# Two attentions in one kernel: rows of the first group loaded earlier, first chunks of scores and their maxima moved into the projection turns ahead, order of the first projection changed

## What is computed

```
block 1:  h = layernorm(x);  q, k, v = h @ Wqkv;  q, k = rotate(q, k)
          a = softmax(causal(q k^T / sqrt(8)));  x = x + (a v) Wo
          x = x + gelu(layernorm(x) W1 + b1) W2 + b2
block 2:  q, k, v = x Wq + bq, ...;  q, k = rotate_half(q, k)
          a = softmax(q k^T / sqrt(8))  (not causal);  x1 = layernorm(x + (a v) Wo + bo)
          top 2 of 8 experts, gelu MLP of width 512 each;  out = layernorm(x1 + moe)
```

## Time and profile before

| | |
|---|---|
| runs | 1601.58, 1604.15, 1609.94 us, median 1604.15 |
| the profiled execution's own time | 1594.96 us |
| its span | 1593.1 us, 36099 instructions |
| mean granted TensorE clock | 0.939 |
| busy: PE, DVE, ACT, POOL | 87%, 76%, 72%, 30% |
| chain that ended last, by engine | PE 42%, DVE 10%, DMA 4%, issue 4%, ACT 3%, POOL 3% |
| DMA queue of SP | 120864 packets, 130.77 MB |

### The profile page before, as it was taken

How to read it: one execution, slowest core, us unless ns; L and a number is a source line. 1 busy time by engine, 2 the same in 40 slices (tenths; PEclk the granted TensorE clock), 3 DMA queues, 4 the chain that set the end, 5 groups by cost and what they waited for, 6 DMA issues and landing times.

```text
span 1593.1 us, 36099 instructions
## 1 busy us (share of the span) xinstructions
PE 1386.2 (87%) x13425; PEld 602.7 (38%) x13425; DVE 1215.1 (76%) x1846; ACT 1143.0 (72%) x2357; POOL 480.9 (30%) x786
## 2 busy tenths in 40 slices
PE   5669999999998899369999999999989998999840
PEld 2323343334333566112222222322322235889730
DVE  6788888888883466799999999999999952523334
ACT  7618888888888566129999998899879986434321
POOL 5413333333333566200000002100222344323455
PEclk9959999999999999659999999999999999999975
DMA  4622112121112353301333331112001405688741
GB/s 139 195 86 75 64 46 70 44 76 52 68 46 88 116 169 116 128 6 48 108 137 125 109 95 37 43 57 91 30 35 48 134 30 152 189 247 258 234 126 56
DMA packets 130256, 158.26 MB, mean 99 GB/s; under 512 B 17313, under 2 KB 103329, under 8 KB 129825
## 3 DMA queue, kind: packets, MB, share of 16 engines
q1 hardware_dynamic: 120864, 130.77, 26.2%
q0 software_dynamic: 9216, 25.18, 4.6%
HBM read 90.90 MB, written 68.96 MB: 100 GB/s over the span
## 4 chain that ended last, share of the span: by engine, by line
PE 42%; DVE 10%; DMA 4%; issue 4%; ACT 3%; POOL 3%; SPq 1%; ACTq 0%; POOLq 0%; DVEq 0%
PE bank L628 16%; PE banks L613 9%; DVE row_max L664 7%; PE banks L585 6%; PE banks L1524 3%; PE banks L1514 3%; DMA sorted_in<-v_all,slots 2%; POOL probs L1332 2%; PE banks L1416 2%; ACT o_sums L724 1%; DMA parts<-sorted_in 1%; PE banks L337 1%; DMA qk_parts<-parts 1%; ACT front L2015 1%; PE bank L1423 0%
## 5 line engine op out<-in xcount | busy, mean ns | idle before, releaser
L664 DVE TENSOR_REDUCE row_max<-banks 128x2 f32<-128x1024 f32 (+3 forms) x896 | 933.7, 1105 | 60.8 <-PE banks L585 32.9
L709 ACT ACTIVATE probs<-banks 128x512 f32<-128x512 f32 (+3 forms) x1792 | 875.7, 553 | 116.4 <-PE banks L613 93.8
L628 PE MATMUL bank<-probs,v_ones 128*32 128x256 f32 (+2 forms) x6656 | 523.2, 386 | 11.9 <-ACT o_sums L724 10.8
L585 PE MATMUL banks<-k_work,q_work 48*128 48x512 bf16 (+3 forms) x1792 | 358.4, 376 | 66.9 <-DVE row_max L664 47.8
L613 PE MATMUL banks<-q_work,k_work 51*128 51x512 bf16 (+3 forms) x1792 | 376.5, 367 | 10.9 <-ACT probs L709 9.9
L613 PEld LDWEIGHTS banks<-q_work,k_work 51*128 51x128 bf16 x1792 | 104.4, 93 | 380.0 <-ACT probs L709 344.4
L628 PEld LDWEIGHTS bank<-probs,v_ones 128*32 128x32 f32 x6656 | 133.7, 108 | 258.1 <-ACT probs L709 174.2
L750 POOL DMA_DIRECT2D heads_out<-o_sums x64 | 36.3, 567 | 470.2 <-ACT o_sums L724 470.2
L2092 ACT ACTIVATE rope<-banks,expert 128x256 f32<-128x256 f32 x184 | 72.0, 474 | 113.5 <-PE banks L1514 113.5
L770 POOL TENSOR_SCALAR_AFFINE_SELECT probs<-probs 128x256 f32<-128x256 f32 x256 | 103.6, 408 | 127.3 <-ACT probs L709 126.5
L585 PEld LDWEIGHTS banks<-k_work,q_work 48*128 48x128 bf16 x1792 | 90.2, 95 | 125.0 <-DVE row_max L664 91.2
(11 more groups left out here) (195 smaller groups left out, 1042.5 us busy)
## 6 DMA issues: line engine op xcount, KB each, us to landing
expert<-expert_rows SPq DMA_DIRECT2D x46, 578.0 KB, 4.4
qk_parts<-parts SPq DMA_DIRECT2D x64, 256.0 KB, 2.7
heads_out<-o_sums POOLq DMA_DIRECT2D x64, 256.0 KB, 3.8
sorted_in<-front SPq DMA_DIRECT2D x21, 512.0 KB, 5.9
q_work<-qk_parts SPq DMA_DIRECT2D x64, 128.0 KB
k_work<-qk_parts SPq DMA_DIRECT2D x64, 128.0 KB
parts<-sorted_in SPq DMA_DIRECT2D x46, 128.0 KB, 4.3
q_work<-qk_parts SPq DMA_DIRECT2D x64, 64.0 KB
```

The source lines that it names most:

```text
L585: last = pe.matmul(to[:, par, 0:width], q[r:r + M0, pair, qt * P:(qt + 1) * P], k[r:r + M0, pair, kh * G:kh * G + width], start=True, stop ...
L628: last = pe.matmul(bank[7][32 * j:32 * j + 32, c0 + c1:c0 + c1 + w], v_ones[i % QB][:, kt, j, :], prob_slots[:, (e + j) % RING, c1:c1 + w] ...
L664: dve.tensor_reduce(row_max[:, :, pair, qt, kh], self.buf_of("chunk", g, c)[:, :, 0:width], AX.X, ALU.max).then_inc(s["chunk_max"], 1)
L709: act.activation(prob_slots[:, e % RING, 0:width], self.ring_bank("exp", e)[:, 0:width], ACT.Exp, scale=SCALE).then_inc(s["exps"], 1)
```

## The change

The chunk and its maximum become methods, so that the stage ahead can call them. EARLY says how many chunks of group 0 it makes: 5 of 24 in the first attention, 6 of 32 in the second. The rest of the first LEAD ones stay where they were.

```diff
+EARLY = {1: 5, 2: 6}
+        LAST_HALVES = (GROUPS - 1, 2 * GROUPS - 1)
+                self.turned = (hT, yT) if a == 1 else (hT, hT)
+            def bank_of(self, which, n):
+                return bank[WO_BANK if n in LAST_HALVES else which]
             def input(self, act, n):
-                if n:
-                    act.wait_ge(s["v"], n)
                 if a == 1:
-                    act.activation(hT[:, :], bank[T_BANK], ...
+                    if n >= 2:
+                        act.wait_ge(s["v"], n - 1)
+                    act.activation(self.turned[n % 2][:, :], self.bank_of(T_BANK, n), ...
-                for c in range(LEAD):
-                    chunk(0, c)
+                for c in range(self.early, LEAD):
+                    self.chunk(pe, 0, c)
```

```diff
 @block.sync
-            for n in range(GROUPS):
-                sp.wait_ge(first["ln"], n + 1)
-                sp.dma_start(tokens(x_ln_d, *divmod(n, HALVES)), f_ln[n % 2]).then_inc(ln_out[n % 2], 16)
-                if n + 3 < GROUPS:
-                    load_first(n + 3)
+            store_ln(0)
+            for n in range(GROUPS):
                 proj[1].store(sp, n, 0)
-                if n >= LOAD_FROM:
-                    if n == LOAD_FROM:
-                        sp.wait_ge(ones_set, 2 * QB)
-                    attend[1].load(sp, n - LOAD_FROM)
+                if n + 1 < GROUPS:
+                    store_ln(n + 1)
+                if n == GROUPS - 3:
+                    sp.wait_ge(ones_set, QB)
+                    sp.wait_ge(rows_set, QB)
+                    attend[1].load(sp, 0)
                 proj[1].store(sp, n, 1)
                 proj[1].store(sp, n, 2)
+            for i in range(1, QB):
+                attend[1].load(sp, i)
 @block.gpsimd
-            for i in range(QB):
-                pool.memset(k_work[HALF + 32:P, i, :], -1.0).then_inc(ones_set, 1)
-            for i in range(QB):
-                pool.memset(v_ones[i][:, :, :, :], 1.0)
+                if n < QB:
+                    ones(n)
+                elif n < 2 * QB:
+                    pool.memset(v_ones[n - QB][:, :, :, :], 1.0)
 @block.tensor
                 proj[1].products(pe, n)
-                proj[1].values(pe, n)
                 if n + 1 < GROUPS:
                     proj[1].turn(pe, n + 1, f_z[(n + 1) % 2])
+                proj[1].values(pe, n)
+                if n == GROUPS - 2:
+                    pe.wait_ge(loaded_masks, 16 * len(masks))
+                    attend[1].chunk(pe, 0, 0)
+            pe.wait_ge(proj[1].s["v_kept"], GROUPS - 1)
+            for c in range(1, EARLY[1]):
+                attend[1].chunk(pe, 0, c)
 @block.vector
             first_moments(0)
+            ones(0)
             first_moments(1)
+            ones(1)
+            ones(2)
                 if n + 2 < GROUPS:
                     first_moments(n + 2)
+                if n == GROUPS - 2:
+                    attend[1].clear(dve)
+                    attend[1].chunk_maximum(dve, 0, 0)
+                if n == GROUPS - 1:
+                    for c in range(1, EARLY[1]):
+                        attend[1].chunk_maximum(dve, 0, c)
                 proj[1].residual(dve, n)
 @block.scalar
-            for i in range(QB):
-                act.activation(k_work[32:HALF, i, :].rearrange("p (a s) -> p a s", s=P),
...
             first_ln(0)
-            first_ln(1)
             for n in range(GROUPS):
-                proj[1].keep(act, n)
                 if n + 1 < GROUPS:
                     proj[1].input(act, n + 1)
+                proj[1].keep(act, n)
                 proj[1].high(act, n)
+                if n + 1 < GROUPS:
+                    first_ln(n + 1)
                 proj[1].middle(act, n)
                 if n + 2 < GROUPS:
                     first_z(n + 2)
-                    first_ln(n + 2)
```

```diff
 @block.sync
-                if LOAD_FROM <= i - 3 < GROUPS:
-                    attend[2].load(sp, i - 3 - LOAD_FROM)
+                if i == GROUPS - 2:
+                    attend[2].load(sp, 0)
+            for i in range(1, QB):
+                attend[2].load(sp, i)
 @block.tensor
+                if i == GROUPS:
+                    pe.wait_ge(mid["gelu"], FC * GROUPS)
+                    attend[2].chunk(pe, 0, 0)
+                    pe.wait_ge(proj[2].s["hT"], 2 * GROUPS - 1)
+                    pe.wait_ge(proj[2].s["v_kept"], 2 * GROUPS - 1)
+                    attend[2].chunk(pe, 0, 1)
+                if i == GROUPS + 1:
+                    for c in range(2, EARLY[2]):
+                        attend[2].chunk(pe, 0, c)
 @block.vector
+                if i == GROUPS + 1:
+                    attend[2].clear(dve)
+                    for c in range(0, 2):
+                        attend[2].chunk_maximum(dve, 0, c)
+                if i == GROUPS + 2:
+                    for c in range(2, EARLY[2]):
+                        attend[2].chunk_maximum(dve, 0, c)
```

More of the change, by code:

```diff
@@ L302, in build @@
         ones_set = sem("ones_set")
+        rows_set = sem("rows_set")
         maxima_cleared = sem("maxima_cleared")
@@ L541, in sp, with free @@
                         self.store_reciprocals(sp, i // HG - 1)
+            def free(self, pe, slot):
+                if slot < CHUNK_BUFS:
+                    return
+                what, g, c = self.slots[slot - CHUNK_BUFS]
+                if what == "chunk":
+                    pe.wait_ge(self.s["chunk_max"], g * self.nc + c + 1)
+                elif what == "product":
+                    pe.wait_ge(end["xc"], HALVES * (g + 1))
+                elif what == "turn":
+                    pe.wait_ge(end["x1T"], HALVES * (g + 1))
+                elif what == "logits":
+                    pe.wait_ge(end["gate"], HALVES * (g + 1))
+                else:
+                    pe.wait_ge(end["slots"], g + 1)
@@ new lines, in chunk @@
+            def chunk(self, pe, g, c):
+                qt, pair, kh, width, masked = self.chunks[c]
+                q, k, to = q_rows[g % QB], k_rows[g % QB], self.buf_of("chunk", g, c)
+                if c == 0:
+                    pe.wait_ge(self.rows_in[g % QB], 16 * ROW_LOADS * (g // QB + 1))
+                self.free(pe, self.slot_of["chunk", g, c])
+                for par in range(2):
+                    r = par * HALF
+                    last = pe.matmul(to[:, par, 0:width], q[r:r + M0, pair, qt * P:(qt + 1) * P],
+                                     k[r:r + M0, pair, kh * G:kh * G + width], start=True, stop=not masked)
+                if masked:
+                    for half in range(2):
+                        for par in range(2):
+                            r, c0 = par * HALF, half * HALF
+                            last = pe.matmul(to[:, par, width - P + c0:width], half_ident[r:r + HALF, half, :],
+                                             later_keys[r:r + HALF, half, c0:P], start=False, stop=half == 1)
+                last.then_inc(self.s["chunk"], 1)
@@ L544, in pe @@
             def pe(self, pe, front=None, between=None, turn=None):
                 s = self.s
[L547 to L562, removed]
@@ L575, in ring_free @@
                         pe.wait_ge(end["x1T"], m + 1)
[L577 to L588, removed]
-                            for par in range(2):
-                                r, c0 = par * HALF, half * HALF
-                                last = pe.matmul(to[:, par, width - P + c0:width], half_ident[r:r + HALF, half, :],
-                                                 later_keys[r:r + HALF, half, c0:P], start=False, stop=half == 1)
-                    last.then_inc(s["chunk"], 1)
                 def maxima(g):
@@ L673, in maxima @@
                                       ALU.max).then_inc(s["maxima"], 1)
[L675 to L678 removed]
+                for c in range(self.early, LEAD):
+                    self.chunk_maximum(dve, 0, c)
                 for i in range(-1, NG):
@@ L687, in dve @@
                         if what == "chunk" and i + ahead < NG:
-                            chunk(i + ahead, n)
+                            self.chunk_maximum(dve, i + ahead, n)
             def act(self, act, between=None):
```

53 lines of the change are left out of this document (28 added, 25 removed).

## The result

The changed kernel takes 1593.4 us (median of 20 runs, 1587.5 to 1602.0), the kernel before 1603.5 (20 runs, 1596.3 to 1615.0): ratio 0.9937, 95% interval 0.9918 to 0.9956, so 10.1 us less, with 7 to 13 in the interval. The profiled execution took 1589.31 us.

The account below looks back on a forecast made before the run. Neither attention has slack on TensorE or VectorE, so only the two seams can gain. Seam 2 -12.7, first attention's start -0.1, hold of the maxima +4.7: -8.1 us from 1604.15, giving 1596.0, range 1585 to 1606.

Parts of the forecast that it names:

- seam 2: Middle stage into second attention: load(0) issued earlier and early chunks beside waits gain 12.7 us, bounds 10.7 to 14.
- the wait at chunk 0: Start of first attention: TensorE waits 9 us for load(0), products(7) behind it; the stall only moves, gain nothing.
- the hold of the maxima: First attention: the maxima's transfer shares DMA engines with load(2), so the first unit is 4.7 us late (3 to 7).
- R: First attention: start of chunk 5's maximum, predicted at 86.6 us where it was 86.65.
- start: rope(0): Start of first projection: memsets no longer ahead of the first root, three on VectorE mostly hidden; rope(0) 2.0 us earlier.
- rope(0) to rope(5): First projection: the new order takes 7.8 us a turn for 8.0, gaining 1.1 us by half 5.
- rope(5) to load(0): First projection: `high`(5) and now x_ln(6) stand before load(0), 8.7 us, so it goes out only 2.6 earlier.
- chunk 0 to R: First attention: from chunk 0 at 74.6 us through rope(7), maxima 1 to 4 and residual(7) to 86.6.
- A: Rival, first attention: the maxima aren't held behind load(2); -12.8 us, 1591.3; chance 0.13.
- B: Rival, first attention: group 0's rows are there when TensorE comes to chunk 0; -16 us, 1588; chance 0.15.
- C: Rival, both seams: each load takes x longer than 13.25 us; slower from x = 2.3, 1610 at 3.8; chance 0.10.
- D: Rival: seam 2 gives only part, through early chunks' cost or a slipping middle stage; about -3.5 us, 1600.5; chance 0.12.

Follow-up runs that it names:

- the repeat: The changed kernel itself timed and profiled once more, with no new edit, against the kernel before: ratio 0.9941, 9.4 us below it.
- the order restored: Changed kernel with chunk 0 and load(2) late, and the first projection's TensorE, ScalarE and SP order as before: 0.987, 20.8 us below the kernel before.
- both edits together: Changed kernel with chunk 0 in the last turn and load(2) behind group 0's maxima transfer: ratio 0.9873, repeated 0.9868, against the kernel before.
- portions of two, load(2) late: Changed kernel, first attention's load(0) issued two transfers a half, load(2) behind group 0's maxima transfer: ratio 0.9903, 15.5 us below the kernel before.

## Why the prediction was right or wrong

It was right in sign and size: 1596.0 predicted, 1593.4 measured; -8.1 against -10.1 with an interval of -13 to -7. Its mechanism held at seam 2, for the wait at chunk 0 and for the hold of the maxima. The path from the start to R was mis-sized: the prediction has -0.1, the trace +2.85. By the landmarks the sum is -6.6, 1.5 us short of the forecast, and the medians lie 2 us beyond it; that the total came so near is in part luck.

| term | predicted | measured |
|---|---|---|
| seam 2 | -12.7 | -13.1 |
| start: rope(0) | -2.0 | -0.8 |
| rope(0) to rope(5) | -1.1 | -0.35; +0.4 in the repeat |
| rope(5) to load(0) (8.3 before) | 8.7 | 10.1; 8.15 in the repeat |
| load(0) to chunk 0 | 13.25 | 13.8 |
| chunk 0 to R | 12.0 | 11.0 |
| R against before (86.55) | -0.1 | +2.85; +1.5 in the repeat |
| hold of the maxima | +4.7 | +3.75 |

**Seam 2.** Right step by step: load(0) at 617.36, which is the 613.4 of the prediction shifted by the 3.9 us that this execution was behind; `high`(13) without a wait for a DMA; 9.6 us by the load, the rest by the chunks.

**"The stall is only moved ... gain nothing."** The place was right (a wait of 9 us at chunk 0 predicted, 10.28 found); the value was not nothing but a loss. The steps that failed are these. *The memsets on VectorE, "one hides before the second x, two in the 5.4 us idle ahead of rope(0)"*: when the start of the products moved up, that idle time shrank with it. Timeline of the start, changed kernel:

```profile
5.49 1.65 POOL L1211 TENSOR_TENSOR first_rstd<-first_var,minus_halves 128x8 f32<-128x8 f32 x1 [4.26 <-DVE first_mean L1618]
5.81 1.76 DVE L1621 MEMSET k_work<- 32x2048 bf16 x1 [0.48 <-issue]
...
10.92 1.76 DVE L1621 MEMSET k_work<- 32x2048 bf16 x1 [0.48 <-issue]
11.28 6.47 PE L344 MATMUL banks<-hT,w_qk 128*128 128x512 f32 x8 [0.95 <-ACT hT L407]
...
13.06 1.76 DVE L1621 MEMSET k_work<- 32x2048 bf16 x1 [0.38 <-issue]
14.86 1.29 DVE L367 TENSOR_TENSOR probs<-banks,rope 128x512 f32<-128x512 f32 x2
```

The products start 2.19 us earlier (13.47 before), rope(0) only 0.80, at the end of the third memset. *The period, "7.8 a turn"*: the three of the five halves that ran at full clock took 7.47, 7.89 and 7.93 us, 7.8 in the mean as forecast; but one, at a granted clock of 0.64, took 9.17, and the five together 39.67 us for 40.02. In the kernel before halves at 0.84 to 0.94 took 7.6 to 8.7. The prediction had no term for the clock there. *"`High`(5) and now x_ln(6) stand before load(0): 8.7"*: the queue was named, its price too low (10.1 us; 8.15 in the repeat, so it varies by 2); the order restored gave R 1.5 us back.

**The hold.** Mechanism and place right, shown by moving load(2) alone and by the packets; 3.75 for 4.7 us, inside the bounds of 3 to 7 (3.2 to 4.8 over the six kernels that have it).

**Rivals.** A (not held) falls by that same run. B (rows there in time) by the wait of 10.28 us. C (each load longer) by 13.8 us: x is 0.55, not 2.3. D (seam 2 gives part) by 13.1.

Six runs can't part 2 us in this kernel, so the seams were settled by landmarks. In the 13 timed versions, the changed kernel among them, the time differs from the landmarks' sum by -4.3 us (both edits together, the repeat) to +3.2 (portions of two, load(2) late), by -3.5 in the changed kernel.

## What to carry to other kernels

A wait that is moved from an engine with nothing behind it into the queue of one that has work is not free: look at what stands behind the waiting instruction, and put the early work last in the stage, not first. When a transfer is moved, ask for each later one whether it needs the same DMA engines, small ones above all: two transfers of 12 KB waited 3.75 us for a load of 768 KB that nobody needed yet. And the idle time in which an added operation is to hide must be measured after the change's own speed-up, not before.

## What the runs showed of the hardware that I had not expected

The granted clock falls in other places in each execution, and takes single stages with it. The stretch from the last top_max of the first attention to `high` of half 13 has the same code in the changed kernel and in the one with both edits together, yet it took 138.2 us (494.66 to 632.90) in the first and 145.8 (484.01 to 629.77) in the repeat of the second; 140.9 in the kernel before. Busy time of this whole stretch, changed kernel, its repeat, then the other:

```profile
494.66:632.90 138.24, 126.23 (x803) 73.64 (x800) 68.29 (x212) 95.30 (x192) 84.37 (x96) 1.00 0.45 137
```

```profile
493.31:636.62 143.31, 132.80 (x803) 73.98 (x800) 68.12 (x212) 95.74 (x193) 84.41 (x96) 0.94 0.44 132
```

```profile
484.01:629.77 145.76, 134.37 (x804) 75.86 (x800) 68.17 (x212) 96.01 (x193) 84.52 (x96) 0.93 0.43 130
```

TensorE has the same 803 or 804 matmuls and is busy 126.2, 132.8 and 134.4 us with them; VectorE, ScalarE and GpSimd are as busy in all three. The first had the higher of the two clock levels (2.4 GHz) throughout, the other two the lower one (1.2 GHz) for part of it. The 14 profiled executions fall in line, but for one that stands a little high: 138.2 us at a granted clock of 1.00 (two of them), 139.5 and 139.6 at 0.99, 140.9 at 0.98 (two), 144.2 at 0.95, 143.3 to 143.4 at 0.94 (three), 145.0 to 145.8 at 0.93 (four). By these rows 0.93 is about 20 us at the lower level and costs 7 us; so, as an estimate, 1 us at the lower level costs a third of a us here.

The rest of the kernel is less clear: from the second attention's first top_max to the end it is 893.7 to 909.7 us at clocks of 0.934 to 0.949, and the changed kernel and its repeat, both at 0.945, are 6.9 us apart. What makes that difference stays open.

The same shows in the times: of the changed kernel's 20 runs the three of highest mean clock (0.941 and 0.942) took 1587.5 to 1590.5 us, the two of lowest (0.933) 1598.1 and 1602.0. So a difference of 5 us between two profiled executions of this kernel means nothing until the stage that it lies in is named. In the first projection of the changed kernel it is the same: a half takes 7.2 to 7.9 us, and 9.2 where the clock falls in it.
